# Attention and mixture of experts on one core: P by V in blocks of four, its normalising moved, V in halves over six steps

## The chip, the core and the metric

The kernel runs on one NeuronCore of a Trainium2 chip. The metric is the device time of one execution in microseconds; the median of three runs is given. The core has TensorE (PE, matrix products), VectorE (DVE), ScalarE (ACT), GpSimd (POOL) and SyncE (SP), which here issues the transfers. Each engine runs its own list of instructions in order; semaphores join the lists.

## The reference

A batch of 16 sequences of 56 tokens attends to 1500 context keys each, with 16 heads of 8 lanes, and then goes through a mixture of 8 experts (top 2) and a shared expert. Cut to what matters here:

```python
q = query @ qw.T + qb ; k = key @ kw.T + kb ; v = value @ vw.T + vb      # 16 heads of 8
scores = einsum('bhqd,bhkd->bhqk', qh * 8 ** -0.5, kh)
scores = where(mask == 0, -1e9, scores)
probs = softmax(scores, axis=-1)
out = einsum('bhqk,bhkd->bhqd', probs, vh) ... @ ow.T + ob
x = x + tanh(g_xattn) * out                                             # query = layernorm(x)
x = x + tanh(g_ffn) * ffn(layernorm(x))                                 # 8 experts, top 2, and a shared one
```

## The kernel before

**Units.** The attention works on one batch element (a unit, number k) at a time, in 12 steps (j = 0 to 11), one for each tile of 128 keys (the last has 92). While unit k turns its own scores into probabilities and products, the first scores of unit k + 1 are made between, and K of unit k + 2. Three buffers of keys, of qrs (the queries) and of v_ext hold the three.

**What a unit of TensorE issues** (pe_unit, L456):
- L376, 24 score matmuls of element k + 1, 8 pairs of heads in 3 chunks of 512, 512 and 476 keys. The table S_ORDER (L246) gives each a step and one of five places in it. They write two banks of PSUM (ring 0 and 1) in turn, and number m waits until VectorE has read number m - 2. VectorE takes the maximum of each (L570), merges them (L579), TensorE turns the row (L384), ScalarE copies it into qrs (L512), and only then may unit k + 1 start.
- L397, one set of eight transposed score matmuls for each step, into two banks (st) in turn; ScalarE takes the exponential of each (L523) into a buffer of probs. With a constant 1 in each head's lanes of v_ext the sum of the probabilities comes out of the same product as P by V.
- L416, P by V: per tile of keys eight matmuls, each on 32 columns of the array, accumulated in pv. Two tiles make a pair: tiles j - 3 and j - 2 in the odd steps 3 to 11, and the last two of the unit before in step 1 (LAG = 2). They come between places 3 and 4 of a step.
- L312, K of element k + 2 in three chunks (steps 0, 1, 2), L321 a small product for masked-out keys (step 3), L350, V of element k + 1 in three chunks of two halves each (steps 4, 5, 6, the halves on both sides of place 2), and L333, the spread of the sums (step 8). These four share one bank, misc (ring 2), so each waits until the one before has been read.

**What reads it.** VectorE: the maxima in the order of S_ORDER, L561 in step 3, the three ops that gather P by V and the sums (L588, L590, L592, "normalising", NORM_STEP = 1), the reciprocal of the sums (L599, RECIP_STEP = 8), then the mask of a later element. ScalarE: L491 copies K, L523 the exponentials, L503 and L505 copy V, L512 the row of maxima. GpSimd splits K in high and low halves (L648, L651), makes qrs (L660) and multiplies by the reciprocal (L669). SyncE loads the context of element k + 3 as soon as V has been made from the buffer (L283), and places masks and keys.

**Buffers of probs.** There are four; the exponential of step j waits for the product of tile j - 4.

**Ends.** A unit -1 makes only scores, K and V; unit 15 has no scores, K or V to make, and takes in the first parts of the output projection (L717) and of the feed-forward part, which fills the time after 415.6 us.

## Time and profile before

| | us |
|---|---|
| median of 3 runs | 521.51 |
| lowest, highest | 521.38, 522.75 |
| profiled execution | 521.78 |
| its span | 520.0 |

| engine | busy us in the span | share |
|---|---|---|
| PE | 475.7 | 91% |
| DVE | 404.6 | 78% |
| ACT | 332.4 | 64% |
| POOL | 161.0 | 31% |

The costliest groups are the maxima (L570, 245.0 us in 384 instructions), the exponentials (L523, 172.6 us in 192) and the score matmuls (L376, 149.9 us in 384). Most of the chain that ended last lies on PE (78%). In a timeline the second column is the length of the record; records overlap within an engine, so what an instruction costs is the distance from its start to the next start.

### The profile page before, as it was taken

The numbers are of one execution on the slowest core, as the hardware profiler recorded it, in microseconds if no ns is written. First come the engines' busy times: TensorE is split into PE (matmuls) and PEld (weight loads), VectorE is DVE, ScalarE is ACT, GpSimd is POOL, SyncE is SP. The second block draws the span as 40 slices with busy tenths as digits, with TensorE's granted clock in tenths as the row PEclk, the third lists the DMA queues.
The fourth block names the chain that finished last, engine by engine and source line by source line (L and its number), as shares of the span: only waits on it lengthen the run. The fifth ranks groups of instructions, "written<-read, shape, count | busy, mean of one in ns | idle before, by whom it ended". The sixth has DMA issues, their size and how long they took to land.

```text
span 520.0 us, 15739 instructions
## 1 busy us (share of the span) xinstructions
PE 475.7 (91%) x6779; PEld 353.0 (68%) x6779; DVE 404.6 (78%) x786; ACT 332.4 (64%) x423; POOL 161.0 (31%) x142
## 2 busy tenths in 40 slices
PE   2483999999999999999999999999999989999993
PEld 1131577776877777786867777687768866777772
DVE  5985677878788778778878787878776768888776
ACT  3411566767666666766676676757656878877872
POOL 4160606244260615335160624426195100000000
PEclk9877899999999999999999999999999989999998
DMA  6599869997977969697987969786500200221001
GB/s 192 177 228 232 166 167 217 248 207 173 224 154 179 199 155 210 174 210 163 203 173 161 218 162 205 177 161 132 109 3 2 85 2 27 56 75 49 3 1 35
DMA packets 41465, 74.28 MB, mean 143 GB/s; under 512 B 4339, under 2 KB 28532, under 8 KB 41397
## 3 DMA queue, kind: packets, MB, share of 16 engines
q1 hardware_dynamic: 40756, 72.48, 62.4%
q8 instruction: 53, 0.87, 0.8%
q10 hardware_dynamic: 640, 0.81, 0.6%
q14 instruction: 16, 0.12, 0.1%
HBM read 24.28 MB, written 0.46 MB: 48 GB/s over the span
## 4 chain that ended last, share of the span: by engine, by line
PE 78%; DVE 9%; ACT 4%; issue 3%; SPq 3%; DMA 3%; DVEq 0%
PE pv L416 16%; PE ring L376 16%; PE st L397 11%; PE ring L350 9%; PE st L892 7%; PE ring L312 6%; PE ring L945 6%; DVE max_part L570 2%; ACT v_ext L503 2%; SPq L1031 2%; DMA o_bias<-in_ob 2%; PE pv L945 2%; PE ring L333 1%; PE ring L384 1%; DVE sums L592 1%
## 5 line engine op out<-in xcount | busy, mean ns | idle before, releaser
L570 DVE TENSOR_REDUCE max_part<-ring 112x1 f32<-112x512 f32 (+1 forms) x384 | 245.0, 676 | 71.4 <-PE ring L376 71.4
L523 ACT ACTIVATE probs<-st 128x896 f32<-128x896 f32 x192 | 172.6, 916 | 73.9 <-PE st L397 71.7
L376 PE MATMUL ring<-keys,qrs 121*112 121x512 f16 (+1 forms) x384 | 149.9, 392 | 11.7 <-POOL qrs L660 5.0
L397 PEld LDWEIGHTS st<-qrs,keys 121*128 121x128 f16 (+1 forms) x1536 | 97.0, 102 | 29.5 <-issue 8.9
L397 PE MATMUL st<-qrs,keys 121*128 121x112 f16 (+1 forms) x1536 | 106.4, 213 | 1.0 <-ACT qrs L512 1.0
L416 PE MATMUL pv<-probs,v_ext 128*32 128x168 f32 (+3 forms) x3072 | 94.3, 262 | 0.3
L416 PEld LDWEIGHTS pv<-probs,v_ext 128*32 128x32 f32 (+1 forms) x3072 | 73.3, 109 | 22.3 <-issue 11.8
L376 PEld LDWEIGHTS ring<-keys,qrs 121*112 121x112 f16 x384 | 49.8, 130 | 45.9 <-issue 22.1
L648 POOL TENSOR_TENSOR k_hi<-k_raw,zero 128x512 f16<-128x512 f32 (+1 forms) x45 | 46.1, 1025 | 87.5 <-ACT k_raw L491 87.5
L350 PE MATMUL ring<-w_qkv,ctxT 128*128 128x128 f32 (+1 forms) x384 | 60.0, 278 | 1.7 <-ACT v_ext L503 0.5
L350 PEld LDWEIGHTS ring<-w_qkv,ctxT 128*128 128x128 f32 (+1 forms) x384 | 56.3, 188 | 6.4 <-ACT v_ext L503 4.4
L491 ACT ACTIVATE k_raw<-ring,biases 128x512 f32<-128x512 f32 (+1 forms) x45 | 30.5, 677 | 41.1 <-PE ring L312 39.2
L920 DVE TENSOR_TENSOR keys<-probs,keys 128x896 f16<-128x896 f32 (+2 forms) x44 | 40.4, 919 | 17.7 <-ACT keys L913 17.4
L651 POOL TENSOR_TENSOR k_lo<-k_raw,k_hi 128x512 f16<-128x512 f32 (+1 forms) x45 | 51.2, 1138 | 3.5
L312 PE MATMUL ring<-ctxT,w_qkv 128*128 128x512 f32 (+1 forms) x94 | 51.8, 636 | 0.4 <-issue 0.4
L669 POOL TENSOR_TENSOR attn<-sums,recip 128x112 f32<-128x112 f32 x15 | 6.3, 422 | 142.2 <-DVE recip L599 142.2
L903 ACT ACTIVATE probs<-st,up_bias 128x896 f32<-128x896 f32 (+2 forms) x44 | 38.3, 869 | 17.7 <-PE st L892 17.4
L892 PE MATMUL st<-keys 128*128 128x512 f16 (+1 forms) x216 | 48.4, 356 | 0.9 <-ACT probs L903 0.9
L503 ACT ACTIVATE v_ext<-ring 128x512 f32<-128x512 f32 (+1 forms) x48 | 27.2, 566 | 26.7 <-PE ring L350 26.7
L945 PEld LDWEIGHTS ring<-keys 128*128 128x128 f16 x612 | 37.6, 100 | 9.1 <-DVE keys L920 2.5
L945 PE MATMUL ring<-keys 128*128 128x128 f16 x612 | 42.5, 222 | 1.3 <-DVE keys L920 1.3
L913 ACT ACTIVATE keys<-probs 128x896 f16<-128x896 f32 (+2 forms) x44 | 35.8, 814 | 1.4
(130 smaller groups left out, 355.6 us busy)
## 6 DMA issues: line engine op xcount, KB each, us to landing
keys<-mask_add SPq DMA_DIRECT2D x30, 750.0 KB, 9.7
ctxT<-in_ctx SPq DMA_DIRECT2D x16, 750.0 KB, 6.2
keys<-k_hi SPq DMA_DIRECT2D x30, 375.0 KB, 7.2
keys<-k_lo SPq DMA_DIRECT2D x30, 375.0 KB, 7.9
mask_raw<-in_mask SPq DMA_DIRECT2D x15, 375.0 KB, 3.8
up_w<-in_up_w SPq DMA_DIRECT2D x9, 256.0 KB, 2.8
down_w<-in_down_w SPq DMA_DIRECT2D x9, 256.0 KB, 3.3
keys<-keys SPq DMA_DIRECT2D x8, 128.0 KB, 2.5
```

Of the source, the lines that this page charges most:

```text
L312: nc.tensor.matmul((first_k[c] if known(k, -1) else misc)[:, 0:width(c)], w_qkv[:, 1, :], ctxT[:, w, chunk(c)], start=True, stop=True).the ...
L350: mm = nc.tensor.matmul(misc[0:m, i * P:(i + 1) * P], ctxT[:, buf(b, 1), j * P:j * P + m], w_qkv[:, 2, :], start=True, stop=True)
L376: nc.tensor.matmul(ring[0:QW, m % 2, 0:width(c)], qrs[0:ROWS, w, p, :, :].rearrange("r h q -> r (h q)"), keys[0:ROWS, w, p, chunk(c)], sta ...
L397: mm = nc.tensor.matmul(st[0:m, j % 2, p // 4, QW * (p % 4):QW * (p % 4 + 1)], keys[0:ROWS, u, p, j * P:j * P + m], qrs[0:ROWS, u, p, :, : ...
L416: mm = nc.tensor.matmul(pv[rows, last * HG * S:last * HG * S + n * S], v_ext[0:m, u, j, VW * h:VW * h + CW], probs[0:m, j % 4, S * h:S * ( ...
L523: nc.scalar.activation(probs[0:m, j % 4, :].rearrange("p (h c) -> p h c", h=2), st[0:m, j % 2, :, 0:HQ // 2], ACT.Exp).then_inc(s["exps_do ...
L570: nc.vector.tensor_reduce(max_part[:, p, c:c + 1], ring[0:QW, m % 2, 0:width(c)], AX.X, ALU.max).then_inc(s["max_read"], 1)
L648: nc.gpsimd.tensor_tensor(k_hi[:, chunk(c)], k_raw[:, chunk(c)], zero[:, :].to_broadcast([P, width(c)]), ALU.add).then_inc(s["k_hi_made"], 1)
L651: nc.gpsimd.tensor_tensor(k_lo[:, chunk(c)], k_raw[:, chunk(c)], k_hi[:, chunk(c)], ALU.subtract).then_inc(s["k_lo_made"], 1)
L892: mm = nc.tensor.matmul(st[:, n % 2, h, 0:cols], split_w[e][:, 0, w, c * P:(c + 1) * P], xn_p[:, x, 4 * P * h:4 * P * h + cols], start=(i ...
L920: nc.vector.tensor_tensor(hid[:, n % HR, 1, cols], hid_raw[n % 3][:, cols], hid[:, n % HR, 0, cols], ALU.subtract).then_inc(s["hid_lo_done ...
L945: mm = nc.tensor.matmul(down_banks[e % 2][t // 4][:, P * (t % 4):P * (t % 4 + 1)], hid[:, n % HR, x, P * t:P * (t + 1)], split_w[e][:, 1, ...
```

## The change

P by V is done in blocks of four tiles: in step 2 (tiles 8 to 11 of the unit before), step 6 (tiles 0 to 3) and step 10 (tiles 4 to 7). probs gets eight buffers, used in turn across units. The three normalising ops move from step 1 to step 3, before the block of step 6, which begins a new accumulation. The spread of the sums goes from step 8 to step 6, ahead of the block, and the reciprocal is issued in step 6 in front of the last maximum of that step. V is made in six steps (4, 5, 7, 8, 9, 10), one half in each, and ScalarE copies a chunk after its second half (steps 5, 8, 10). S_ORDER is written anew: the places of the 24 score matmuls are now 2, 3, 3, 2, 2, 2, 3, 2, 2, 2, 1 in the steps 0 to 10 (before 2, 3, 2, 2, 3, 3, 3, 1, 2, 2, 1). The projection in unit 14 goes from step 10 to 11. Some waits are added. Of the tables the lines that differ in their constants are shown.

```diff
WIDE = CG * HG
+PB = 8
+QUAD = 4
 VPAD = VW * (H - 1) + CW
...
         neg_max = sb("neg_max", [QW, PAIRS], F16)
-        probs = sb("probs", [P, 4, HQ])
+        probs = sb("probs", [P, PB, HQ])
         recip = sb("recip", [P, 2, S])
...
+        def slot(k, j):
+            return (KT * k + j) % PB
         def known(k, below):
...
-        S_ORDER = ((0, 0), (0, 1), (1, 0), (1, 1), (1, 4), (2, 0), (2, 1), (3, 1), (3, 4), (4, 1), (4, 2), (4, 3),
+        S_ORDER = ((0, 0), (0, 1), (1, 0), (1, 1), (1, 4), (2, 0), (2, 1), (2, 4), (3, 1), (3, 3), (4, 1), (4, 2), (5, 1), (5, 2),
         S_SLOTS = {place: (m,) for m, place in enumerate(S_ORDER)}
...
         SCORES = PAIRS * NCH
-        K_STEPS, ANY_STEP, V_STEPS, ATTN_STEP, TURN_STEP = (0, 1, 2), 3, (4, 5, 6), 8, 11
-        NORM_STEP, RECIP_STEP = 1, 8
+        K_STEPS, ANY_STEP, ATTN_STEP, TURN_STEP = (0, 1, 2), 3, 6, 11
+        V_STEPS = {4: (0, 0), 5: (0, 1), 7: (1, 0), 8: (1, 1), 9: (2, 0), 10: (2, 1)}
+        PV_STEPS = {2: 8, 6: 0, 10: 4}
+        NORM_STEP, RECIP_STEP = 3, 6
...
                     pe.wait_ge(s["recip_done"], k - 1)
-                elif not known(k, 0):
+                if not known(k, 0):
                     pe.wait_ge(s["v_stored"], NCH * (k + 1))
...
             if has(k, 1):
-                pe.wait_ge(s["v_stored"], NCH * (k + 2))
+                pe.wait_ge(s["v_stored"], NCH * (k + 1) + 1)
             else:
+                pe.wait_ge(s["v_stored"], NCH * B)
                 pe.wait_ge(s["recip_done"], k - 1)
...
                     pe.wait_ge(s["recip_done"], k - 1)
+                    pe.wait_ge(s["v_stored"], NCH * (k + 1))
             elif not half:
                 pe.wait_ge(s["v_stored"], NCH * (k + 1) + c)
+                if c == 1 and has(k, -1):
+                    pe.wait_ge(s["recip_done"], k)
             for i in range(2 * half, 2 * half + 2):
...
                                       v_ext[0:m, u, j, VW * h:VW * h + CW],
-                                      probs[0:m, j % 4, S * h:S * (h + n)],
+                                      probs[0:m, slot(k, j), S * h:S * (h + n)],
                                       start=(j == 0 and not last), stop=(j == KT - 1), skip_group_check=True)
...
-        LAG = 2
-        def pe_pv_pair(pe, b, j):
-            k, u, t = b
-            if j % 2 and j > LAG and has(k, 0):
-                for i in (j - LAG - 1, j - LAG):
-                    pe_pv(pe, b, i)
-            if j == LAG - 1 and has(k, -1):
-                for i in range(KT - LAG, KT):
-                    pe_pv(pe, (k - 1, buf(b, -1), None), i)
+        LAG = QUAD
+        def pe_pv_quad(pe, b, j):
+            k, u, t = b
+            if j not in PV_STEPS or not has(k, -1 if j == min(PV_STEPS) else 0):
+                return
+            late = j == min(PV_STEPS)
+            for i in range(PV_STEPS[j], PV_STEPS[j] + QUAD):
+                pe_pv(pe, (k - 1, buf(b, -1), None) if late else b, i)
...
-            if (k, j) == (B - 2, 10):
+            if (k, j) == (B - 2, 11):
+                pe.wait_ge(s["v_stored"], NCH * B)
                 pe.wait_ge(s["attn_stored"], B - 2)
...
                         pe_k(pe, b, K_STEPS.index(j))
-                    pe_slot(pe, b, j, 0)
+                pe_slot(pe, b, j, 0)
                 if has(k, 0):
...
                     pe_attn(pe, b)
-                if j in V_STEPS:
-                    if has(k, 1):
-                        pe_v(pe, b, V_STEPS.index(j), 0)
-                    pe_slot(pe, b, j, 2)
-                    if has(k, 1):
-                        pe_v(pe, b, V_STEPS.index(j), 1)
+                if j in V_STEPS and has(k, 1):
+                    pe_v(pe, b, *V_STEPS[j])
+                pe_slot(pe, b, j, 2)
                 pe_slot(pe, b, j, 3)
-                pe_pv_pair(pe, b, j)
+                pe_pv_quad(pe, b, j)
                 pe_slot(pe, b, j, 4)
...
             act.wait_ge(s["st_made"], KT * k + j + 1)
-            if j >= 4 or not known(k, 1):
-                act.wait_ge(s["pv_done"], KT * k + j - 3)
-            nc.scalar.activation(probs[0:m, j % 4, :].rearrange("p (h c) -> p h c", h=2),
+            if KT * k + j >= PB:
+                act.wait_ge(s["pv_done"], KT * k + j - PB + 1)
+            nc.scalar.activation(probs[0:m, slot(k, j), :].rearrange("p (h c) -> p h c", h=2),
                                  st[0:m, j % 2, :, 0:HQ // 2], ACT.Exp).then_inc(s["exps_done"], 1)
...
                     act_exp(act, b, j)
-                if j in V_STEPS and has(k, 1):
-                    act_v(act, b, V_STEPS.index(j))
+                if j in V_STEPS and V_STEPS[j][1] and has(k, 1):
+                    act_v(act, b, V_STEPS[j][0])
                 if j == TURN_STEP and has(k, 1):
...
                 for m in S_STEPS[j][j == ANY_STEP:] if has(k, 1) else ():
+                    if j == RECIP_STEP and m == S_STEPS[j][-1] and has(k, -1):
+                        dve_recip(dve, b)
                     dve_max(dve, b, m)
...
                     dve_ready_tiles(dve, j)
-                if j == RECIP_STEP and has(k, -1):
+                if j == RECIP_STEP and has(k, -1) and not has(k, 1):
                     dve_recip(dve, b)
...
```

How the order moves on VectorE, in steps 0 to 10 of one middle unit. Before:

```order
L570 TENSOR_REDUCE max_part<-ring 112x1 x5
L588 TENSOR_TENSOR own_pv<-pv,c_f 128x168
L590 COPY sums<-pv 128x56
L592 TENSOR_REDUCE sums<-own_pv 128x56
L570 TENSOR_REDUCE max_part<-ring 112x1 x3
L561 SCALAR_TENSOR_TENSOR any_key<-ring,halves 128x112
L570 TENSOR_REDUCE max_part<-ring 112x1 x13
L599 RECIPROCAL recip<-ring 128x112
L570 TENSOR_REDUCE max_part<-ring 112x1 x3
L579 TENSOR_REDUCE neg_max<-max_part 112x8
```

Now:

```order
L579 TENSOR_REDUCE max_part<-ring 112x1 x9
L570 SCALAR_TENSOR_TENSOR any_key<-ring,halves 128x112
L579 TENSOR_REDUCE max_part<-ring 112x1
L597 TENSOR_TENSOR own_pv<-pv,c_f 128x168
L599 COPY sums<-pv 128x56
L601 TENSOR_REDUCE sums<-own_pv 128x56
L579 TENSOR_REDUCE max_part<-ring 112x1 x6
L608 RECIPROCAL recip<-ring 128x112
L579 TENSOR_REDUCE max_part<-ring 112x1 x8
L588 TENSOR_REDUCE neg_max<-max_part 112x8
```

Of the 24 maxima (L570 before, L579 now) five stood ahead of the normalising ops and 19 behind; now ten stand ahead, and the op on any_key stands right before the tenth. The reciprocal has six maxima ahead of it since normalising, and eight behind it, where it had three.

TensorE from step 10 (before: from the score matmul ahead of it) to the row of maxima in step 11 of a middle unit. Before (a row with x2 on pv is a part of a tile, which has eight matmuls; "..." stands for the rest of the block):

```order
L376 MATMUL ring<-keys,qrs 112x476
L397 MATMUL st<-qrs,keys 128x112 x8
L376 MATMUL ring<-keys,qrs 112x476
L397 MATMUL st<-qrs,keys 92x112 x8
L416 MATMUL pv<-probs,v_ext 32x168 x2
L416 MATMUL pv<-probs,v_ext 32x56 x2
...
L384 MATMUL ring<-ident_h,neg_max 1x112 x8
```

Now:

```order
L388 MATMUL ring<-keys,qrs 112x476
L409 MATMUL st<-qrs,keys 128x112 x8
L388 MATMUL ring<-keys,qrs 112x476
L362 MATMUL ring<-w_qkv,ctxT 128x128
L362 MATMUL ring<-w_qkv,ctxT 92x128
L428 MATMUL pv<-probs,v_ext 32x168 x2
L428 MATMUL pv<-probs,v_ext 32x56 x2
...
L409 MATMUL st<-qrs,keys 92x112 x8
L396 MATMUL ring<-ident_h,neg_max 1x112 x8
```

The pair that stood between the last transposed scores (the row with 92x112) and the row of maxima (L384 before, L396 now) is gone from there; a half of V and then the block of four stand in front of the last transposed scores.

## Rows read from the trace of the kernel before

**Rows 1.** Windows: us, busy time of each engine, granted clock of PE, DMA share, GB/s.

```profile
239.00:262.00 23.00, 22.78 (x355) 17.25 (x356) 18.61 (x33) 15.41 (x20) 8.69 (x8) 1.00 0.86 185
...
420.00:424.00 4.00, 4.00 (x31) 2.68 (x29) 3.54 (x15) 1.95 (x3) 0.00 (x0) 0.61 0.00 2
```

**Rows 2.** Timeline, PE, unit 9: start us, length us, engine, line, what.

```profile
262.00 0.39 PE L376 MATMUL ring<-keys,qrs 121*112 121x512 f16 x1
262.23 0.56 PE L397 MATMUL st<-qrs,keys 121*128 121x112 f16 x8
262.62 0.38 PE L376 MATMUL ring<-keys,qrs 121*112 121x512 f16 x1
262.84 1.03 PE L312 MATMUL ring<-ctxT,w_qkv 128*128 128x512 f32 x2
263.70 0.38 PE L376 MATMUL ring<-keys,qrs 121*112 121x512 f16 x1
...
264.32 0.38 PE L376 MATMUL ring<-keys,qrs 121*112 121x512 f16 x1
264.63 0.98 PE L416 MATMUL pv<-probs,v_ext 128*32 128x168 f32 x32
265.53 0.42 PE L376 MATMUL ring<-keys,qrs 121*112 121x512 f16 x1
...
268.08 0.42 PE L376 MATMUL ring<-keys,qrs 121*112 121x512 f16 x1
```

**Rows 3.** Timeline, DVE, same unit.

```profile
262.43 1.30 DVE L570 TENSOR_REDUCE max_part<-ring 112x1 f32<-112x512 f32 x2 [0.66 <-PE ring L376]
...
266.60 0.32 DVE L588 TENSOR_TENSOR own_pv<-pv,c_f 128x168 f32<-128x168 f32 x1
...
267.35 1.89 DVE L570 TENSOR_REDUCE max_part<-ring 112x1 f32<-112x512 f32 x3
269.15 0.27 DVE L561 SCALAR_TENSOR_TENSOR any_key<-ring,halves 128x112 f16<-128x112 f32 x1
...
280.39 0.85 DVE L599 RECIPROCAL recip<-ring 128x112 f32<-128x112 f32 x1
```

**Rows 4.** Timeline, PE and ACT, steps 4 and 5 of the same unit.

```profile
270.90 0.61 PE L350 MATMUL ring<-w_qkv,ctxT 128*128 128x128 f32 x4
...
271.35 0.38 PE L376 MATMUL ring<-keys,qrs 121*112 121x512 f16 x1
271.55 0.60 ACT L503 ACTIVATE v_ext<-ring 128x512 f32<-128x512 f32 x1 [0.41 <-PE ring L350]
...
272.20 0.71 PE L350 MATMUL ring<-w_qkv,ctxT 128*128 128x128 f32 x4
```

**Rows 5.** Timeline, PE and ACT, first exponential and the turn to the next unit.

```profile
262.82 0.92 ACT L523 ACTIVATE probs<-st 128x896 f32<-128x896 f32 x1
...
282.05 1.72 ACT L523 ACTIVATE probs<-st 128x896 f32<-128x896 f32 x2 [0.92 <-PE st L397]
...
283.84 1.13 PE L312 MATMUL ring<-ctxT,w_qkv 128*128 128x512 f32 x2
283.94 0.91 ACT L512 ACTIVATE qrs<-ring 1x896 f16<-1x896 f32 x1 [0.18 <-PE ring L384]
...
285.00 0.39 PE L376 MATMUL ring<-keys,qrs 121*112 121x512 f16 x1
```

**Rows 6.** Windows, L416 alone, two tiles of four in a row: PE, PEld, clock.

```profile
413.62:414.39 0.77, 0.77 (x32) 0.71 (x36) 1.00 0.08 21
```

**Rows 7.** First score matmuls of units 0, 1 and 14; window of unit 15.

```profile
55.11 0.63 PE L376 MATMUL ring<-keys,qrs 121*112 121x512 f16 x1
...
77.41 0.39 PE L376 MATMUL ring<-keys,qrs 121*112 121x512 f16 x1
...
377.33 0.39 PE L376 MATMUL ring<-keys,qrs 121*112 121x512 f16 x1 [1.09 <-ACT qrs L512]
...
401.50:415.60 14.10, 13.93 (x338) 12.12 (x338) 9.32 (x34) 11.10 (x13) 3.13 (x3) 1.00 0.27 78
```

More of the change, by code:

```diff
@@ L243, in width @@
             return chunk(c).stop - c * CH
-        S_ORDER = ((0, 0), (0, 1), (1, 0), (1, 1), (1, 4), (2, 0), (2, 1), (3, 1), (3, 4), (4, 1), (4, 2), (4, 3),
-                   (5, 2), (5, 3), (5, 4), (6, 1), (6, 2), (6, 3), (7, 4), (8, 1), (8, 3), (9, 1), (9, 4), (10, 1))
+        S_ORDER = ((0, 0), (0, 1), (1, 0), (1, 1), (1, 4), (2, 0), (2, 1), (2, 4), (3, 1), (3, 3), (4, 1), (4, 2), (5, 1), (5, 2),
+                   (6, 0), (6, 1), (6, 4), (7, 1), (7, 2), (8, 1), (8, 2), (9, 1), (9, 2), (10, 1))
         S_SLOTS = {place: (m,) for m, place in enumerate(S_ORDER)}
```

## The prediction

> **What bounds the kernel now.** I read the windows by engine first, then the timeline of TensorE through one batch, then VectorE and ScalarE beside it. The kernel runs thirteen like units (batches 1 to 13), each 23.00 us from one first score matmul (L376, "S" below) to the next: 262.00 to 285.00 [rows 2, 5]. TensorE is busy for 22.78 of them, VectorE for 18.61, ScalarE for 15.41 [rows 1]. Its idle time hides in start-to-start distances: a piece that takes longer than its like has waited. Prices: an S .22 (262.62 to 262.84), the eight transposed scores of a step ("ST", L397) .39, a K chunk .86 [rows 2], half a V chunk .45 [rows 4], a pair of P by V tiles .90 and .31 rather than .22 from the S in front to its start [rows 2]. What waits: the S at 268.08 [rows 2], which comes .73 after the maximum at 267.35 that frees its bank [rows 3], some .27 late; the V half at 272.20, .65 behind the copy at 271.55 [rows 4], some .24 late; and the K at 283.84, after which S needs 1.16 instead of .86, since it waits for the copy of the row of maxima at 283.94 (S is 1.06 behind it) [rows 5]. With a tenth in step 5, .9 us of 23.0 are waits; TensorE's own work is 22.1. So TensorE bounds a unit, with VectorE close behind.
>
> The Trainium skill ("Perfetto Trace Analysis", section "Identifying the Most-Contended Engine") says that matmul busy time is a poor measure and that the busy share of weight loads should be taken for TensorE. That would be 17.25 of 23.00, a quarter of the unit free, and edits of TensorE's work would then be worth nothing (521.8 again); the start distances, which show .9 of waiting, speak against it, and the rest of this text does not use it.
>
> **What the blocks of four save.** Before, six pairs stand in a unit; after, three fours. In a row of four at 413.62 two tiles begin within .77 [rows 6], so a tile costs .385, and a pair's .90 holds .13 of getting out; with .09 of getting in, a block costs .22 beside its tiles, plus a few hundredths on the S behind it. A four is then .90 + .77 = 1.67 (bounds: 4 x .385 = 1.54, and twice .90 = 1.80; I take 1.67, since the row of four shows no seam). Three blocks fewer: 3 x .25 = .75. I take .5: the last pair before runs straight into the row of maxima and pays only .81 until that, and ops behind a wait pay a few hundredths again. TensorE's own work falls from 22.1 to about 21.6.
>
> **What the new order costs.** I lay one unit out. Rules: a maximum starts .43 behind its S (262.00, 262.43) and at least .60 behind the maximum before it (267.35, three to 269.15) [rows 2, 3]; S number m starts no sooner than .73 after the start of maximum m-2 (two banks). The any-product's VectorE op (.27 long) costs the row about .2, since records overlap there; the three normalising ops .75 (266.60 to 267.35) [rows 3]. S0 is at 0.
> - Steps 0 to 2: S0 0, S1 .62, S2 1.70, S3 2.32. S4 stands straight behind S3 now and needs maximum 2 (2.13) + .73 = 2.86 instead of 2.54: **.32 of wait**. S5 3.88, S6 4.49, block 4.80 to 6.47, S7 6.47. VectorE has run dry under the block; its next maximum, 7, is at 6.90.
> - Steps 3 to 6: nine S (7 to 15), the any-product and the normalising ops all go in here. VectorE: 7 at 6.90, 8 at 7.51, any 8.1, 9 at 8.3, normalising 8.9, 10 at 9.65, 11 at 10.25, 12 at 10.85, 13 at 11.48. TensorE between S7 and S15 has eight S, four ST, two V halves and the small any-product, 1.76 + 1.56 + .90 + .1 = 4.3; VectorE has 8 x .60 + .2 + .75 = 5.75. So S9 waits .2, S11 .1, **S12 .74** (for maximum 10, which the normalising ops push back), S14 .3, and S15 is at 12.2. In the kernel before, the normalising ops lie in step 1 and the pairs are spread, so that one wait of .27 is all there.
> - Block of step 6: attention's spread product (no row; four records like a V half's, narrower: .4) and .09 put it at 12.9 to 14.6. The reciprocal (.85) [rows 3] and maxima 14, 15 lie under it and cost nothing: before, it took its place between maxima, with the same result.
> - Steps 7 to 9: S, V half, S, ST are 1.25 for two maxima (1.2): no wait on VectorE. V's third chunk begins at 17.9 but the copy of the second stands behind exp 8 (ST at 16.1, exp .59 later as 262.23 to 262.82, next op .81 on, as in the two at 282.05) [rows 2, 5] at 17.5, plus .65: 18.1, .2 of wait. Last S 19.2, V half, block 19.9 to 21.6.
> - The turn: the last ST now stands behind the block, at 21.6. Its exp is at 22.2, the copy of the maxima's row cannot start before 22.2 + .81 = 23.0, and S0 of the next unit is 1.06 on: 24.1. TensorE is ready at 21.6 + .39 + .49 + .86 = 23.35: **.7 of wait** in place of .3. Before, a pair stood between the last ST and the maxima's row and gave ScalarE time.
>
> Waits add up to 2.6 against .9: 21.6 + 2.6 = 24.2 by sum, 24.1 by the layout. A full unit costs **+1.1 us**, 13 of them +14.3.
>
> **What moves at no cost.** K and masks: the load of the context waits for all of V and goes from step 6 to step 10, some 5 us later, still before the mask's copies; it is needed more than a unit later. P goes to eight buffers, so exps never wait for a block; the extra wait_ge on V and the reciprocal are met 1 us or more early (reciprocal at 13.4, V's third half at 15.4).
>
> **The ends.** Unit 0 (55.11 to 77.41, 22.3) [rows 7] loses its step-2 block and normalising: laid out in the same way VectorE carries S15 to 10.1, and the unit is 2.5 shorter than a full one, 21.5 and .3 for its slow first ops (the S at 55.11 takes .63, that at 262.00 .39): -.5. Unit 14 (from 377.33) has no K; its output projection covers the turn: +.2. Unit 15 takes 14.1 [rows 7] and has neither S nor V; four ST in a row between two blocks run at ScalarE's .81 instead of .39, twice, and the four at the end starts behind the last of them: about +1.5 (bounds 0 and 2.5). Together +1.2. What follows 415.6 is the same work.
>
> Sum: 14.3 + 1.2 = 15.5. The profiled execution took 521.78 (span 520.0), the median is 521.51: **537.0 us**.
>
> **Rivals.**
> - *VectorE does not bind (faster).* Place: S7 to S15 and the turn. If the maxima came .46 apart instead of .60 in steps 3 to 6 (or the normalising ops ran beside them), 1.1 of the waits would go and the unit would be 23.0; below that the change wins. With all the new waits gone a unit is 22.5: 13 x -.5 and +1.2 at the ends, 516. Against it: three in a row at 267.35 keep .60 whatever stands ready. 7%.
> - *Half of the waits.* The turn is no later than before: -.4 x 13, 532. It lies in my range.
> - *No change* (within .3%, which is what a measurement of this kernel can tell from none): the waits come to 1.4 in all instead of 2.6. 3%.
> - *The granted clock falls.* TensorE now stands still 2.6 us of each 24. The clock was 1.00 through the units, and .61 over 420 to 424 [rows 1], some 3.1 us at 1.2 GHz, about 1.6 us lost. Once per unit it would be 13 x 1.6 = 21 more, 558. The longest new stop is .7, and the stretch 401.50 to 415.60 with its small stops kept 1.00 [rows 7]; 3%. [...]
> - *A late transfer.* Context and mask now run together at the end of a unit. Queues were busy .86 [rows 1]; 750 KB more in front of the keys' copies is some 4 us at 185 GB/s, and the keys have about that left. If they came 1 us late per unit: 550. 2%.
>
> **Numbers.** Forecast with its bounds (block 1.54 to 1.80, that is -.4 to +.4 a unit, ends 0 to 2.5) 529 to 546: 83%; the other cases 17%. Range 529 to 546. Faster 7%, same 3%, slower 90%.
>
> **What the profile would show.** Blocks of four of 1.6 to 1.7 us, three a unit, right for the saving. TensorE's L388 waiting for L579 some 1.5 us a unit, in steps 3 to 6, most at the first S behind normalising; unit length 24.1; .7 idle before a unit's first S, with the copy of the maxima's row straight behind the last exp. I am wrong if units are 22.5 to 23, if VectorE has idle time in steps 3 to 6, or if the granted clock leaves 1.00 within the units.

## The result, and the profile after

The changed kernel takes 545.07 us (median of 4 runs, 543.95 to 547.13), the kernel before 521.44 in the same comparison (4 runs, 521.31 to 522.75). The ratio is 1.0447, with a 95% interval of 1.0419 to 1.0476: slower, 8 us above the forecast of 537.0 and inside its range. The profiled execution took 543.95, its span is 542.1; before it was 521.78 and 520.0. It is the fastest of the four, so the account of 22.1 us below leaves some 1.5 of the 23.6 between the medians without one.

From the page of the kernel after, busy time by engine and the chain that ended last:

```profile
PE 476.0 (88%) x6779; PEld 349.3 (64%) x6779; DVE 403.0 (74%) x786; ACT 330.7 (61%) x423; POOL 160.9 (30%) x142
...
PE 60%; DVE 19%; issue 7%; ACT 7%; SPq 3%; DMA 3%; DVEq 0%; ACTq 0%
```

The work is the same, within .1% on TensorE (475.7 before) and .5% on the other two. The span is 22.1 longer, and the chain says whose time was added: TensorE has 60% of it instead of 78%, VectorE 19% instead of 9%, ScalarE 7% instead of 4%. The waits (engine and what it was about to do, what it waited for: us, times, longest) name the places:

```profile
DVE max_part L579 <- PE ring L388: 90.8, 92, 4.2
...
PEld ring L388 <- DVE max_part L579: 44.6, 101, 1.1
...
PE ring L388 <- ACT qrs L521: 7.9, 14, 1.5
```

The weight load of a score matmul is what stands first in TensorE's queue when a bank is not free; it waited for a maximum 17.0 us in the kernel before, and 44.6 now. VectorE in turn waits more for scores, 90.8 instead of 71.4: both engines wait for each other more than they did.

The windows of one full unit and of unit 15 (us, busy time of PE, PEld, DVE, ACT and POOL, granted clock, DMA share, GB/s). The first answers to [rows 1], the second to [rows 7]:

```profile
150.89:175.35 24.46, 22.97 (x355) 17.11 (x356) 18.52 (x33) 15.34 (x21) 8.69 (x8) 1.00 0.78 169
...
421.52:438.52 17.00, 14.80 (x370) 12.79 (x371) 10.14 (x40) 10.89 (x13) 0.42 (x1) 1.00 0.15 47
```

Twelve of the thirteen full units last 24.46 us, where they lasted 23.00; the other lasts 25.79, because of a single stop. TensorE is busy for 22.97 of them (22.78 before), so its idle share went from 1% to 6% and its granted clock stayed at 1.00. The account of the 22.1 us: 13 x 1.46 = 19.0; stops of single units +.4 (1.3 here, .6 and .3 before); unit 0 22.21 instead of 22.30; unit 14 24.70 instead of 24.19, +.5; unit 15 17.00 instead of 14.1, +2.9; a start .2 later and a rest .8 shorter (103.6 instead of 104.4). That rest is 103.6 in every other trace too, those of the kernel before with an edit among them, so the .8 belongs to the one execution and not to the change.

One unit on TensorE from its first score matmul (L388) on; it answers to [rows 2]. Columns: start, length, engine, line, what:

```profile
150.89 0.39 PE L388 MATMUL ring<-keys,qrs 121*112 121x512 f16 x1 [0.49 <-ACT qrs L521]
...
153.20 0.38 PE L388 MATMUL ring<-keys,qrs 121*112 121x512 f16 x1
153.76 0.42 PE L388 MATMUL ring<-keys,qrs 121*112 121x512 f16 x1 [0.17 <-DVE max_part L579]
...
155.74 1.74 PE L428 MATMUL pv<-probs,v_ext 128*32 128x168 f32 x64
157.41 0.42 PE L388 MATMUL ring<-keys,qrs 121*112 121x512 f16 x1
...
160.27 0.56 PE L409 MATMUL st<-qrs,keys 121*128 121x112 f16 x8
161.35 0.42 PE L388 MATMUL ring<-keys,qrs 121*112 121x512 f16 x1 [0.53 <-DVE max_part L579]
...
162.06 0.92 PE L388 MATMUL ring<-keys,qrs 121*112 121x512 f16 x2
...
163.22 0.42 PE L388 MATMUL ring<-keys,qrs 121*112 121x512 f16 x1
...
163.96 1.74 PE L428 MATMUL pv<-probs,v_ext 128*32 128x168 f32 x64
```

And VectorE under it, which answers to [rows 3]:

```profile
155.24 1.30 DVE L579 TENSOR_REDUCE max_part<-ring 112x1 f32<-112x512 f32 x2 [0.33 <-PE ring L388]
157.87 1.30 DVE L579 TENSOR_REDUCE max_part<-ring 112x1 f32<-112x512 f32 x2 [1.33 <-PE ring L388]
159.09 0.27 DVE L570 SCALAR_TENSOR_TENSOR any_key<-ring,halves 128x112 f16<-128x112 f32 x1
159.27 0.68 DVE L579 TENSOR_REDUCE max_part<-ring 112x1 f32<-112x512 f32 x1
159.87 0.32 DVE L597 TENSOR_TENSOR own_pv<-pv,c_f 128x168 f32<-128x168 f32 x1
...
160.62 3.76 DVE L579 TENSOR_REDUCE max_part<-ring 112x1 f32<-112x512 f32 x6
164.29 0.85 DVE L608 RECIPROCAL recip<-ring 128x112 f32<-128x112 f32 x1
```

Read the two together. S4 (153.76) stands .56 behind S3 (153.20) instead of .22. Then comes the block of four, 155.74 to 157.41, 1.67 us. VectorE has two maxima to do under it (155.24 and, .61 on, 155.85), and then nothing until 157.87: the 1.33 of idle time that this row carries. From the second of the two maxima at 157.87 (for S8, at 158.06) on it works without a gap to the reciprocal at 164.29: eight maxima, the any-product's op and the three normalising ops, from 159.87 to 160.62. TensorE is held to its pace: the score matmul at 161.35 (S12) starts .73 behind the maximum at 160.62, and stands 1.08 behind the transposed scores at 160.27, which cost .39. The second of the two score matmuls in the row at 162.06 (S14, at 162.56) is held in the same way, by the maximum two before it: it stands .50 behind S13 instead of .22. S15 (163.22) follows its transposed scores in .40, so it does not wait any more, and behind it come the spread product and the second block (163.96).

The end of the same unit, PE and ACT, which answers to [rows 5]:

```profile
171.06 1.74 PE L428 MATMUL pv<-probs,v_ext 128*32 128x168 f32 x64
172.73 0.59 PE L409 MATMUL st<-qrs,keys 121*92 121x112 f16 x8
173.25 0.55 PE L396 MATMUL ring<-ident_h,neg_max 112*1 112x112 f16 x8
...
173.36 0.91 ACT L532 ACTIVATE probs<-st 92x896 f32<-92x896 f32 x1 [1.38 <-PE st L409]
...
173.74 1.13 PE L320 MATMUL ring<-ctxT,w_qkv 128*128 128x512 f32 x2
...
174.30 0.91 ACT L521 ACTIVATE qrs<-ring 1x896 f16<-1x896 f32 x1
...
175.35 0.39 PE L388 MATMUL ring<-keys,qrs 121*112 121x512 f16 x1 [0.49 <-ACT qrs L521]
```

The block at 171.06 comes ahead of the last transposed scores (172.73). Their exponential starts at 173.36, the copy of the row of maxima only at 174.30, and the next unit's first S 1.05 later. From K (173.74) to S it is 1.61, where it was 1.16 and K alone takes .86.

### The profile page after: what moved, and what is told of

It reads as the page before. It is cut to its first block, busy times and chain, and to the rows that moved or that the text cites. A ratio compares the mean times of both kernels' runs of the same rounds, so it can differ in the third digit from the quotient of the medians.

```text
span 542.1 us, 15751 instructions
## 1 busy us (share of the span) xinstructions
PE 476.0 (88%) x6779; PEld 349.3 (64%) x6779; DVE 403.0 (74%) x786; ACT 330.7 (61%) x423; POOL 160.9 (30%) x142
## 4 chain that ended last, share of the span: by engine, by line
PE 60%; DVE 19%; issue 7%; ACT 7%; SPq 3%; DMA 3%; DVEq 0%; ACTq 0%
PE pv L428 14%; DVE max_part L579 11%; PE ring L388 11%; PE st L409 8%; PE st L903 7%; PE ring L956 5%; PE ring L320 5%; PE ring L362 4%; ACT qrs L521 3%; DMA o_bias<-in_ob 2%; ACT probs L532 2%; ACT v_ext L512 2%; SPq L1042 2%; PE pv L956 1%; PE ring L342 1%
## 5 line engine op out<-in xcount | busy, mean ns | idle before, releaser
L579 DVE TENSOR_REDUCE max_part<-ring 112x1 f32<-112x512 f32 (+1 forms) x384 | 243.2, 677 | 90.8 <-PE ring L388 90.8
L532 ACT ACTIVATE probs<-st 128x896 f32<-128x896 f32 x192 | 175.4, 918 | 123.4 <-PE st L409 123.4
L388 PE MATMUL ring<-keys,qrs 121*112 121x512 f16 (+1 forms) x384 | 150.9, 395 | 31.3 <-DVE max_part L579 12.1
L388 PEld LDWEIGHTS ring<-keys,qrs 121*112 121x112 f16 x384 | 49.6, 130 | 76.9 <-DVE max_part L579 44.6
L428 PE MATMUL pv<-probs,v_ext 128*32 128x168 f32 (+3 forms) x3072 | 83.6, 261 | 0.0
L428 PEld LDWEIGHTS pv<-probs,v_ext 128*32 128x32 f32 (+1 forms) x3072 | 70.9, 109 | 11.7 <-issue 3.4
L362 PEld LDWEIGHTS ring<-w_qkv,ctxT 128*128 128x128 f32 (+1 forms) x384 | 55.1, 188 | 6.9 <-ACT v_ext L512 5.2
L956 PEld LDWEIGHTS ring<-keys 128*128 128x128 f16 x612 | 36.5, 98 | 9.2 <-DVE keys L931 2.9
L671 POOL TENSOR_TENSOR qrs<-queries,any_key 121x896 f16<-121x896 f16 x16 | 30.4, 1902 | 33.4 <-DVE any_key L570 33.4
```

Of the source, the lines that this page charges most:

```text
L362: mm = nc.tensor.matmul(misc[0:m, i * P:(i + 1) * P], ctxT[:, buf(b, 1), j * P:j * P + m], w_qkv[:, 2, :], start=True, stop=True)
L388: nc.tensor.matmul(ring[0:QW, m % 2, 0:width(c)], qrs[0:ROWS, w, p, :, :].rearrange("r h q -> r (h q)"), keys[0:ROWS, w, p, chunk(c)], sta ...
L428: mm = nc.tensor.matmul(pv[rows, last * HG * S:last * HG * S + n * S], v_ext[0:m, u, j, VW * h:VW * h + CW], probs[0:m, slot(k, j), S * h: ...
L532: nc.scalar.activation(probs[0:m, slot(k, j), :].rearrange("p (h c) -> p h c", h=2), st[0:m, j % 2, :, 0:HQ // 2], ACT.Exp).then_inc(s["ex ...
L579: nc.vector.tensor_reduce(max_part[:, p, c:c + 1], ring[0:QW, m % 2, 0:width(c)], AX.X, ALU.max).then_inc(s["max_read"], 1)
L956: mm = nc.tensor.matmul(down_banks[e % 2][t // 4][:, P * (t % 4):P * (t % 4 + 1)], hid[:, n % HR, x, P * t:P * (t + 1)], split_w[e][:, 1, ...
```

## The experiments

Times are medians; the kernel before had a median of 522.0 us beside the first two groups of runs and 521.8 beside the last. "Unit" is the length of a full unit in the profiled execution.

### How much of the loss is VectorE's

**The changed kernel with maxima over half of the columns.**

```diff
-            nc.vector.tensor_reduce(max_part[:, p, c:c + 1], ring[0:QW, m % 2, 0:width(c)], AX.X,
+            nc.vector.tensor_reduce(max_part[:, p, c:c + 1], ring[0:QW, m % 2, 0:width(c) // 2], AX.X,
                                     ALU.max).then_inc(s["max_read"], 1)
```

> The changed kernel, but every maximum of VectorE reads only half of its columns (256 and 238 instead of 512 and 476), so the row maximum is that of half the keys; all else is as it was. Theory V (VectorE's row of maxima, started dry by the block of step 2, is what the score matmuls wait for in steps 1 to 6): the waits of the score matmuls in steps 1 to 6, 1.6 us of a unit's 24.46, go; a unit is 22.9 and the time about 523. Rival T (the loss is in the turn alone: last exponential, copy, first score): those waits were cover, the unit stays near 24.4, 543 to 545. Rival B (the blocks of four are slower in themselves): also near 24.4.

**The same edit on the kernel before.**

> Control: the kernel before with the same halved maxima (row maximum over half the keys). Theory V: only its .37 us of waits on VectorE can go, a unit 23.0 to 22.6, about 516. Beside the first run it also gives what the fours are worth once VectorE is out of the way: theory V says the changed kernel's unit is then about as long as this one's, plus .4 for the turn, minus .5 for the blocks.

One run of each: 525.54 us and a unit of 23.12 for the changed kernel, 516.28 and 22.69 for the one before. With one run a time says little here (in the changed kernel's, one single unit is 3.5 longer than the others); what the two show is the unit, the length that most units of a trace share. Windows of one unit of each:

```profile
148.79:171.91 23.12, 22.51 (x355) 17.10 (x356) 13.05 (x33) 15.35 (x21) 8.70 (x8) 1.00 0.85 183
```

```profile
122.46:145.15 22.69, 22.57 (x356) 17.19 (x356) 13.23 (x33) 15.40 (x20) 8.69 (x8) 1.00 0.88 188
```

VectorE's busy time falls to 13.05 and 13.23, and TensorE's is alike. Taking VectorE's pace away gives the changed kernel 1.34 us a unit and the kernel before .31, so 1.03 of the 1.46 hang on VectorE's pace. The other .43 stays with fast maxima. The turn is still there in that trace: from K (193.42) to the next unit's first S (195.03) it is 1.61, against 1.16 in its counterpart (143.99 to 145.15), which is .45. I had expected the two units to be about alike, .4 for the turn and .5 back from the blocks. They are .43 apart: some .3 of the waits for VectorE is left in the changed one (S12 stands .64 behind its transposed scores instead of .39, S4 .07 late), and the blocks give back less than .5.

### How much the turn costs

**The third block behind the last transposed scores, in step 11.**

```diff
-        PV_STEPS = {2: 8, 6: 0, 10: 4}
+        PV_STEPS = {2: 8, 6: 0, 11: 4}
```

> The changed kernel with its third block (tiles 4 to 7) in step 11, behind the last transposed scores, instead of step 10. Theory V plus T in part (the turn costs .5 of the 1.46 us that a unit has lost, since the last exponential stands in front of the copy of the maxima): the copy no longer waits for the exponential, a unit is 24.0, the time about 538.5. If the turn is covered by something else: 545, no change.

536.44 us (534.67 to 539.16), ratio 1.0283 (1.0247 to 1.0319), unit 23.79. The turn of one unit:

```profile
169.57 1.74 PE L428 MATMUL pv<-probs,v_ext 128*32 128x168 f32 x64
171.15 0.56 PE L396 MATMUL ring<-ident_h,neg_max 112*1 112x112 f16 x8
...
171.75 0.91 ACT L521 ACTIVATE qrs<-ring 1x896 f16<-1x896 f32 x1 [0.84 <-PE ring L396]
...
172.80 0.40 PE L388 MATMUL ring<-keys,qrs 121*112 121x512 f16 x1
```

The exponential now runs under the block (at 169.98), and the copy starts .60 behind the row of maxima (171.15). From K (171.64) to S it is 1.16, as before. A unit gets .67 back: .45 is this distance, the rest seams, since from the last V half to the row of maxima it is 2.5 us here and 2.72 in the changed kernel (170.53 to 173.25). So the turn is .45 to .67 of the loss. With VectorE's 1.03 that is 1.48 to 1.70 of waits and seams against a loss of 1.46: up to .24 of what the blocks save is left in the changed unit. No run has both edits, so this sum takes it that the two add; the turn of 1.61 with halved maxima speaks for it.

### Whether VectorE's hole under the first block can be filled

**The first block as two halves around the score matmul behind it.**

```diff
             for i in range(PV_STEPS[j], PV_STEPS[j] + QUAD):
+                if late and i == PV_STEPS[j] + 2:
+                    pe_slot(pe, b, j, 4)
                 pe_pv(pe, (k - 1, buf(b, -1), None) if late else b, i)
...
-                pe_slot(pe, b, j, 4)
+                if j != min(PV_STEPS) or not has(k, -1):
+                    pe_slot(pe, b, j, 4)
```

> The changed kernel, but the block of step 2 is two pairs with the score matmul (2, 4) between them instead of behind them; one more seam of .25. Theory V (VectorE starts its full row of steps 3 to 6 late because the block keeps the next score from it): the row starts .75 earlier and the unit is 23.75, the time about 535. Rival: the row is not what binds, or the length of the block does not matter: the seam is paid, 24.7, 548.

550.4 us (548.03 to 551.02), ratio 1.0535 (1.0504 to 1.0566), unit 24.70: slower than the changed kernel. My theory's 535 was wrong, and the rival's unit of 24.7 came out. PE and DVE around the block:

```profile
157.18 0.42 PE L388 MATMUL ring<-keys,qrs 121*112 121x512 f16 x1
157.54 0.98 PE L428 MATMUL pv<-probs,v_ext 128*32 128x168 f32 x32
...
157.64 0.69 DVE L582 TENSOR_REDUCE max_part<-ring 112x1 f32<-112x512 f32 x1 [0.56 <-PE ring L388]
...
158.85 0.38 PE L388 MATMUL ring<-keys,qrs 121*112 121x512 f16 x1
...
159.27 0.69 DVE L582 TENSOR_REDUCE max_part<-ring 112x1 f32<-112x512 f32 x1 [0.93 <-PE ring L388]
```

Its maximum did come earlier: S7 at 157.18, read at 157.64, 6.2 into the unit instead of 7.0. But then VectorE stands still again for .93, for the next score matmul is at 158.85, behind the second half of the block; its maximum at 159.27 is 7.84 into the unit, where the same one stood at 7.60. The row without gaps that holds TensorE until the second block begins with that maximum, so it moved later by .24, and the unit grew by .24. That is the price of one seam, as the rival had it; that the row binds all the same is shown by the halved maxima, not by this run. One score matmul in the middle of the hole only cuts it in two, and pays a second seam. What counts is when the stream of scores starts again.

### Whether normalising in the row matters

**Normalising in step 5.**

```diff
-        NORM_STEP, RECIP_STEP = 3, 6
+        NORM_STEP, RECIP_STEP = 5, 6
```

> The changed kernel with the three normalising ops behind step 5 instead of step 3 on VectorE. Theory V (what counts is the sum of VectorE's work between the block of step 2 and the block of step 6): the waits are pushed to later scores of the same stretch and the unit stays at 24.46, at best .3 less since the last one or two scores need not wait for the ops, 540 to 545. Rival N (it is the place of the normalising in front of the maximum that S12 waits for, .74): that wait goes, 23.7, about 534.

542.18 us (541.29 to 543.9), ratio 1.0383 (1.0347 to 1.0419), unit 24.38. The wait at S12 is gone (S12 is 9.78 into the unit instead of 10.46), and S15 is .73 earlier. But the spread product now waits for the sums, and the block behind it starts 12.99 into the unit instead of 13.07. The wait moved to the other end of the same row. The rival, by which the place of these ops costs .75, is out.

### Whether the fours or the placements lose

**The kernel before with blocks of four in the steps 2, 6 and 10, eight buffers and normalising in step 3, its S_ORDER, V and reciprocal kept.**

```diff
...
-        NORM_STEP, RECIP_STEP = 1, 8
+        NORM_STEP, RECIP_STEP = 3, 8
...
-        LAG = 2
+        LAG = 4
...
-            if j % 2 and j > LAG and has(k, 0):
-                for i in (j - LAG - 1, j - LAG):
+            if j in (6, 10) and has(k, 0):
+                for i in range(j - 6, j - 2):
                     pe_pv(pe, b, i)
-            if j == LAG - 1 and has(k, -1):
+            if j == 2 and has(k, -1):
...
```

> The kernel before with nothing but the fours: blocks in the steps 2, 6 and 10, eight buffers of probabilities, the normalising in step 3; score matmuls, V and the reciprocal where they were. Theory V: the old order has eleven scores and V in the steps 3 to 6, the reciprocal in step 8 stands in the row too, and the unit is longer than with the new order, 25 us or more, 552; the new order then gave part of it back. Rival O (the new order of scores and V is what costs): the fours alone save their seams, 22.5, 515.

554.14 us (552.92 to 559.17), ratio 1.064 (1.0577 to 1.0703), unit 25.12. Fours with the later normalising, on the old placements, cost 2.1 a unit; the rest of the change takes .7 of it back. What the later normalising is worth there by itself, no run shows.

**The changed kernel with pairs again**, in the steps 1, 3, ... 11, normalising in step 1.

```diff
-QUAD = 4
+QUAD = 2
...
-        PV_STEPS = {2: 8, 6: 0, 10: 4}
-        NORM_STEP, RECIP_STEP = 3, 6
+        PV_STEPS = {1: 10, 3: 0, 5: 2, 7: 4, 9: 6, 11: 8}
+        NORM_STEP, RECIP_STEP = 1, 6
```

> The changed kernel with the six pairs back (steps 1, 3, 5, 7, 9 and 11, normalising in step 1); order of scores, V in halves, reciprocal and eight buffers as changed. Theory V: the new order puts its scores so that blocks come after them; with pairs in between, VectorE gets its scores late in other places and the unit stays near 24.3, 543. Rival B (the fours by themselves are what costs): the unit returns to 23.0 to 23.3, 522 to 526.

541.59 us (541.35 to 541.85), ratio 1.0368 (1.0337 to 1.0398), unit 24.32. So the new placements lose 1.32 with pairs too, but at other places. Two rows of its TensorE, with the idle time before them and what ended it:

```profile
157.80 0.42 PE L388 MATMUL ring<-keys,qrs 121*112 121x512 f16 x1 [0.50 <-DVE max_part L579]
...
166.50 0.68 PE L362 MATMUL ring<-w_qkv,ctxT 128*128 128x128 f32 x4 [0.45 <-DVE recip L608]
```

The score matmul at 157.80 waits behind a maximum that normalising pushed back (.87 from the one in front instead of .22), and a V half at 166.50 waits for the reciprocal, since both want the bank misc (.82 instead of .22). Together that is some 1.25, against the one wait of .27 in [rows 2], so about 1.0 of the 1.32; the rest is spread over small distances. The fours on the old places lose 2.1 and the new places with pairs 1.3: neither half of the change is good by itself, and no sum of the two parts gives 1.46. Blocks and places have to be counted together.

### Fours with places made for them

The account so far says what a unit needs: two scores straight in front of a block and two straight behind it, so that VectorE has work under it and finds work after it, and the last block behind the last transposed scores. So I wrote S_ORDER anew, moved the first block to step 1 and the third to step 11, and merged the maxima in step 11.

```diff
-        S_ORDER = ((0, 0), (0, 1), (1, 0), (1, 1), (1, 4), (2, 0), (2, 1), (2, 4), (3, 1), (3, 3), (4, 1), (4, 2), (5, 1), (5, 2),
-                   (6, 0), (6, 1), (6, 4), (7, 1), (7, 2), (8, 1), (8, 2), (9, 1), (9, 2), (10, 1))
+        S_ORDER = ((0, 3), (0, 4), (1, 0), (1, 2), (1, 4), (1, 4), (2, 0), (3, 0), (3, 4), (4, 0), (5, 1), (5, 2),
+                   (6, 1), (6, 2), (6, 4), (7, 0), (8, 0), (8, 1), (8, 3), (9, 1), (9, 2), (10, 1), (11, 0), (11, 2))
...
-        PV_STEPS = {2: 8, 6: 0, 10: 4}
+        PV_STEPS = {1: 8, 6: 0, 11: 4}
...
-                if j == TURN_STEP - 1 and has(k, 1):
+                if j == TURN_STEP and has(k, 1):
```

> Fours kept, placed by what the runs show of VectorE: block of step 2 in step 1, where the row of maxima has the least behind it, third block in step 11 under which the last maxima, the merge and the turn lie, two scores moved to step 11, three behind the blocks, the first two scores behind the first transposed scores of a unit. Theory V: the waits on VectorE in steps 3 to 6 fall from 1.3 us to some .4, the turn is .3 again, the seams stay saved: unit 22.3 to 22.6, 511 to 515, faster than both kernels. Rival (fours cost VectorE more idle time than their seams save wherever they stand): 23.0 or more, 522 and up.

518.34 us (7 runs, 517.32 to 520.19), ratio 0.9927 (0.9905 to 0.9949), unit 22.58: faster than the kernel before by .7%. The unit is what I expected, the time is 3 us above it: the first S of unit 0 comes at 56.32 instead of 55.11, and unit 15 takes 17.2, as in the changed kernel, which I had not counted.

### Two smaller causes, each alone

**The kernel before with the copy of the row of maxima in two halves**, the first of which lets S0 and four of the transposed scores go.

```diff
-                pe.wait_ge(s["max_copied"], k + 1)
+                pe.wait_ge(s["max_copied" if m else "half_copied"], k + 1)
...
+            for x in range(2):
+                nc.scalar.activation(qrs[ONEROW:ONEROW + 1, buf(b, 1), 4 * x:4 * x + 4, :, :]
+                                     .rearrange("r p h q -> r (p h q)"),
+                                     ring[ONEROW:ONEROW + 1, x, 0:4 * QW],
+                                     ACT.Copy).then_inc(s["max_copied" if x else "half_copied"], 1)
```

> The kernel before, with the copy of the row of maxima in two halves, one for each bank; the first score matmul and the first four transposed ones of a unit wait for the first half alone. Theory T (before, .30 us of a unit is a wait for this copy at the turn): that wait goes, a unit is 22.7, 13 to 15 times .3, 517.5. Rival (the wait only moves to the second score or the exponential): 521.5, no change.

521.71 us (11 runs, 520.13 to 523.32), ratio 0.9996 (0.9985 to 1.0008), unit 23.00: no change. PE and ACT at the turn:

```profile
146.35 1.12 PE L312 MATMUL ring<-ctxT,w_qkv 128*128 128x512 f32 x2
...
146.45 0.96 ACT L515 ACTIVATE qrs<-ring 1x448 f16<-1x448 f32 x2 [0.18 <-PE ring L384]
...
147.31 0.38 PE L376 MATMUL ring<-keys,qrs 121*112 121x512 f16 x1
...
147.51 0.69 ACT L493 ACTIVATE k_raw<-ring,biases 128x512 f32<-128x512 f32 x1
...
147.92 0.38 PE L376 MATMUL ring<-keys,qrs 121*112 121x512 f16 x1
148.25 1.13 PE L312 MATMUL ring<-ctxT,w_qkv 128*128 128x512 f32 x2
```

S0 does come earlier, .96 behind K instead of 1.16. But the copy of K stands behind the second half (147.51, .20 after S0, where it started with S0 before), and K's second chunk, which uses the same bank, comes .74 behind that copy: .33 behind S1 instead of .22, and S2 is 1.90 from S0 instead of 1.71. What one wait gave, the next took.

**The changed kernel, in unit 15 normalising ahead of the layer norm.** In unit 15, step 3 of VectorE's order has the second part of a layer norm (13 short ops, the last at 426.82, and L798) in front of normalising; in the kernel before normalising stood ahead of them. Rows of the changed kernel, DVE and PE:

```profile
427.00 0.57 PE L409 MATMUL st<-qrs,keys 121*128 121x112 f16 x8 [0.61 <-ACT probs L532]
...
427.03 1.63 DVE L798 TENSOR_SCALAR attn<-x_tok,ln_mv,ln_rstd 128x128 f32<-128x128 f32 x6
...
427.81 0.57 PE L409 MATMUL st<-qrs,keys 121*128 121x112 f16 x8 [0.24 <-ACT probs L532]
...
428.57 0.32 DVE L597 TENSOR_TENSOR own_pv<-pv,c_f 128x168 f32<-128x168 f32 x1
...
429.54 0.62 PE L342 MATMUL ring<-sums,c_f 128*128 128x56 f32 x4 [1.16 <-DVE sums L601]
```

L597 comes only behind L798, and the spread product at 429.54 waits for L601; without that wait it would stand .41 behind the transposed scores at 427.81, at 428.2.

```diff
-                if j == NORM_STEP and has(k, -1):
+                if j == (2 if k == B - 1 else NORM_STEP) and has(k, -1):
                     dve_norm(dve, b)
```

> The changed kernel, but in unit 15 alone VectorE normalises in step 2, ahead of the layer norm of the first tokens, instead of in step 3 behind it. Unit 15 took 17.0 us against 14.1 before. Theory L (1.4 of these 2.9 us are the spread product in step 6 waiting for normalising that is queued behind the layer norm on VectorE): unit 15 takes 15.6, the time falls by 1.4 to 543.6. Rival (the exponentials alone set unit 15): no change, 545.

543.97 us (541.75 to 545.67), ratio 1.0421 (1.039 to 1.0453); unit 15 15.67 instead of 17.00. DVE and PE:

```profile
426.63 0.33 DVE L597 TENSOR_TENSOR own_pv<-pv,c_f 128x168 f32<-128x168 f32 x1 [1.21 <-PE pv L428]
...
428.86 0.57 PE L409 MATMUL st<-qrs,keys 121*128 121x112 f16 x8 [0.24 <-ACT probs L532]
429.27 0.61 PE L342 MATMUL ring<-sums,c_f 128*128 128x56 f32 x4
```

L597 now starts at 426.63, and the spread product stands straight behind the transposed scores (428.86 to 429.27). The mechanism and the 1.3 us show in the trace; in the time, 545.07 and 543.97 lie within each other's scatter, so there it is not shown.

**All of it together**: the placed fours, the split copy with the first S at (0, 0), and the early normalising in unit 15.

> The fours placed as in the run with the third block in step 11 and the first in step 1, plus the two edits of this call: the copy of the maxima's row in halves with the first score in front again, and the early normalising of unit 15. Theories T and L: a unit of 22.58 becomes 22.2 to 22.3, unit 15 gets 1.4 to 2 shorter, 518.3 becomes 512. Rival: VectorE binds by now in this layout and an earlier first score only lengthens its waits: 22.5, 516.

516.51 us (4 runs, 516.37 to 517.09), ratio 0.9899 (0.9885 to 0.9912): 1.0% faster than the kernel before, and faster than the changed one. One unit:

```profile
144.61:167.20 22.59, 22.41 (x357) 16.93 (x356) 18.62 (x33) 14.88 (x22) 8.69 (x8) 1.00 0.82 189
```

The unit is 22.58, with VectorE as busy as in the kernel before (18.62 and 18.61). Unit 0 takes 21.53 and starts at 55.33. My 512 took the split copy for a gain of .3 a unit; the unit stayed at 22.58, as the rival had it (22.5, 516). Unit 15 takes 16.49 instead of 17.17, .7 shorter and not the 1.4 to 2 that I had counted; in the placed fours the spread product waited only .74 for the sums (at 404.92), against 1.16 in the changed kernel, so .7 was all that the early normalising could give. S2 is 1.91 from S0 (144.61 to 146.52), as in the kernel before with the same edit, which ran beside it and gained nothing either.

## Why the prediction came out as it did

**What held.** The direction and the mechanism: VectorE runs dry under the first block, then nine maxima, the any-product and normalising come in one row, and TensorE keeps its pace. S4 waits .34 (.32 foretold), S9 some .3 (.2), S11 .07 (.1), S12 .69 (.74), S14 .28 (.3), the copy of V's second chunk holds the third by .21 (.2), and the block of four takes 1.67, as the row of four in [rows 6] gave with one way in and out. The reciprocal and the maxima under the second block cost nothing. Half-column maxima put a number on the part that waits for VectorE: 1.34 in the changed unit, .31 in the one before. By the layout the waits on VectorE were .32 + .2 + .1 + .74 + .3 = 1.66; in the trace they come to some 1.7, and with halved maxima .3 of that is left.

**What was too small.** A unit is 24.46, not 24.1: +1.46 instead of +1.1, and the term is mis-sized, not the mechanism. The waits came out as summed: 1.7 on VectorE, .21 on V's copy and .75 at the turn are 2.6. TensorE's own work is the rest, 21.8, where I had 21.6: the blocks save some .25 of the 22.1, not .5. The layout by hand, which ended at 24.06 before rounding, shows the places:
- *The turn.* I put the copy of the row .81 behind the last exponential, the distance of two exponentials in [rows 5]. It is .94 (173.36 to 174.30), and the exponential itself starts .63 behind the transposed scores instead of .59. That is .17 of the .40 between 24.06 and 24.46. The kernel before has no copy close behind an exponential, so no row of it could have told. It is not copies as such: V's copy stands .81 behind an exponential of 128 keys (167.72 to 168.53 in the changed kernel), as a second exponential does. Whether the 92 keys in front or the one row behind makes the .94 is not shown.
- *The small distances.* An instruction behind a wait passes the next in .26, not .22 (161.35 to 161.61; the kernel before has the same, 268.08 to 268.34), and from a V half to a block it is .53 (170.53 to 171.06), not .45. They bring the last transposed scores to 21.84 into the unit instead of 21.6, which is the other .24. I had allowed for "a few hundredths" in the saving of a block and left them out of the layout.

13 x .36 = 4.7 of the 6.6 us between my 15.5 and the 22.1 of the span; unit 15 is 1.4, units 0 and 14 .4 and .3, stops .4, and start and tail give .6 back.

**Unit 15: +2.9 instead of +1.5.** The step that failed is that I moved the normalising ops in a full unit and did not ask what stands ahead of them in unit 15. ScalarE's pace is what I said it would be: with normalising ahead of the layer norm the unit takes 15.67, +1.6. The other 1.3 are the three ops queued behind 13 short ones and L798 on VectorE. This was to be had from the kernel's text.

**That the range held was luck.** The ends together cost +3.3, above the bounds of 0 to 2.5 that I had set. With the bounds that the prediction names, +.4 a unit and 2.5 for the ends, the sum goes to 521.5 + 19.5 + 2.5 = 543.5 at most; the range said 546 and gives no source for the 2.5 above that. The median of 545.07 lies in just that part, and one of the four runs (547.13) lies outside the range.

**Units 0 and 14.** Unit 0 gave .1 instead of .5, unit 14 cost .5 instead of .2. The .4 of unit 0 may be nothing: in the run with the early normalising in unit 15, which has the same instructions in unit 0, it takes 22.88 instead of 22.21. Unit 14 takes 24.70 there too, which speaks against chance for its .5. Its reason stays open: no run took it alone.

**The rivals.** VectorE does bind (516 is out): with short maxima the unit falls by 1.34. Half of the waits (532) is out by the turn, which is later by .45 where that rival left it alone. No fall of the clock: it stayed at 1.00 through every full unit, with two stops of .5 to .7 in each, and over 232.00 to 238.00, where the single stop of 1.97 lies. The Trainium skill ("TensorE: Matmul & The Clock Gate", section "Why this matters for your kernels") warns of idle gaps between bursts; no trace here shows a fall for stops of these lengths. No transfer came late: no row of TensorE waits for a transfer within the units.

The busy share of weight loads, the other measure that was weighed, moved from 17.25 to 17.11 us a unit while the unit grew by 1.46: it saw nothing of what happened. The start distances saw all of it. That bears against half of the rule of the Trainium skill ("Perfetto Trace Analysis", section "Identifying the Most-Contended Engine"), which judges TensorE by this share together with the share of peak arithmetic, for a kernel with matmuls as short as these; the second share was not worked out here. By the same rule VectorE is the most contended engine before, 18.61 against 17.25 of weight loads. That points at the engine whose pace the changed kernel waits for, but in the kernel before halving the maxima gave only .31 of 23.00.

**Where the saving went.** With places made for them the same fours give 22.58 against 23.00, .42, where I had taken .5 for the saving. (That kernel moves the scores too, so the .42 belongs to both.) In the changed kernel some .25 of it is left beside the waits.

## What to carry to other kernels

When two engines pass work through two banks, a long block on the one starves the other after two pieces (here 1.67 us against two maxima of .60), and the engine that was starved then works at its own pace until it has caught up; what the block saves must be set against that. Lay such a unit out by hand with the start-to-start distances of each engine, and check the turn, where the last exponential, the copy and the next unit's first product follow on each other. A wait that an edit removes is worth only the distance to what is late next, so look at that before you count it, and go through the first and last units by themselves: there other work stands ahead in the queues.

## What the runs showed of the hardware that I had not expected

- On ScalarE a copy of a row (1 x 896) starts .94 us behind an exponential of 92 x 896, while two exponentials of 128 x 896 stand .81 apart, and so do such an exponential and a copy of V (128 x 512).
- A block of four tiles of P by V takes 1.67 us up to the next score matmul or transposed scores and 1.58 up to the row of maxima, with no seam inside; two of them in a row at the end of unit 15 take 3.21 (410.86 to 414.07, in the placed fours).
- Getting from a V half into such a block costs .53 instead of the .45 between the half and a score matmul; behind a wait an instruction's successor comes .26 after it instead of .22.
- Single units are longer by .1 to 3.5 us, in ten of the thirteen traces, and the places are not random. In the changed kernel, in the run with the split block and in the one with the early normalising, it is the same score matmul (S10 of unit 7) that comes some 2 us late; the kernel before, two of its edited versions and the run with pairs have theirs in units 5 and 10. The one of the changed kernel, for which no releaser shows:

```profile
234.79 0.42 PE L388 MATMUL ring<-keys,qrs 121*112 121x512 f16 x1 [1.97 <-issue]
```

Its cause stays open; no run was made for it.
